# A graph layer's feed groups: ScalarE in place of VectorE makes the one-hots with which node scores are looked up

## The reference

```
h = relu(layernorm(x))
edge_h = concat([h[src], edge_attr], axis=1)
edge_m = edge_h @ a.T
edge_e = exp(-leaky_relu(edge_m @ a_2[0], 0.2))
e_rowsum = segment_sum(edge_e, src)            # 0 is replaced by 1e-12
h_prime  = segment_sum(edge_e[:, None] * edge_m, src)
out = x + h_prime / e_rowsum[:, None]
```

## Time and profile before

| | |
|---|---|
| device time, median of 3 runs | 1207.09 us (1204.01 to 1208.95) |
| the profiled execution's own time | 1210.7 us |
| its span | 1208.9 us |
| mean granted TensorE clock | 0.72 of full speed |
| busy: VectorE / GpSimd / TensorE / ScalarE | 71% / 64% / 52% / 48% |

### The profile page before, as it was taken

One profiled execution on the slowest core, in us unless ns is written; L12 is line 12 of the kernel. 1 busy time (PEld: TensorE's weight loads), 2 busy tenths in 40 slices (PEclk: granted clock), 3 DMA queues, 4 the chain that ended last, 5 costly groups with the idle time before them and its releaser, 6 DMA issues. The chain is left out here.

```text
span 1208.9 us, 22334 instructions
## 1 busy us (share of the span) xinstructions
PE 626.6 (52%) x5452; PEld 528.9 (44%) x5453; DVE 857.9 (71%) x2932; ACT 585.9 (48%) x2008; POOL 768.1 (64%) x814
## 2 busy tenths in 40 slices
PE   1671018223767028211546077771275488889887
PEld 0561015223656016211535056661264477678766
DVE  5856798876858988843546999873465768834677
ACT  1664020445666040542555034982465309978656
POOL 2006737577777777777777777777777777777000
PEclk9785558556877558555677578985587559979998
DMA  9939959589895652757879385974977529399583
GB/s 299 330 135 351 369 185 331 199 251 393 262 334 160 218 165 87 247 177 267 300 247 305 103 289 185 369 255 160 363 235 232 171 82 282 124 312 289 214 269 108
DMA packets 188561, 291.76 MB, mean 241 GB/s; under 512 B 19288, under 2 KB 125879, under 8 KB 188215
## 3 DMA queue, kind: packets, MB, share of 16 engines
q1 hardware_dynamic: 143940, 162.33, 41.3%
q10 hardware_dynamic: 19442, 75.36, 18.5%
q0 software_dynamic: 25088, 53.04, 12.3%
HBM read 159.04 MB, written 131.61 MB: 240 GB/s over the span
## 5 line engine op out<-in xcount | busy, mean ns | idle before, releaser
L507 POOL DMA_INDIRECT ordered_rows<-feed,dest x784 | 761.5, 971 | 352.7 <-issue 246.2
L755 PE MATMUL psum<-back,hots 128*128 128x129 f32 x2128 | 329.3, 312 | 36.2 <-DVE hots L1056 27.1
L755 PEld LDWEIGHTS psum<-back,hots 128*128 128x128 f32 x2128 | 293.8, 218 | 76.5 <-issue 74.1
L631 ACT ACTIVATE apart<-lanes,back 128x128 bf16<-128x128 bf16 x532 | 169.4, 389 | 236.1 <-PE psum L755 197.6
L725 PE MATMUL psum<-score_parts,place_hot 128*128 128x50 bf16 x2352 | 101.1, 206 | 276.3 <-DVE place_hot L976 257.0
L588 ACT ACTIVATE feed<-feed 128x128 f32<-128x128 f32 (+1 forms) x784 | 238.7, 387 | 0.0
L725 PEld LDWEIGHTS psum<-score_parts,place_hot 128*128 128x128 bf16 x2352 | 92.5, 111 | 286.2 <-DVE place_hot L976 265.1
L976 DVE TENSOR_SCALAR place_hot<-place_rows,lane 128x1024 bf16<-128x1024 bf16 (+1 forms) x98 | 50.1, 511 | 188.6 <-SPq L378 179.0
L580 ACT ACTIVATE feed<-leaky 128x8 f32<-128x8 f32 (+1 forms) x98 | 20.4, 208 | 325.6 <-DVE leaky L1008 325.6
L985 DVE SCALAR_TENSOR_TENSOR junk<-feed,psum 128x128 bf16<-128x128 f32 x784 | 169.9, 280 | 0.0
L1039 DVE TENSOR_TENSOR acc<-acc,psum 128x387 f32 (+1 forms) x133 | 73.5, 553 | 58.8 <-PE psum L755 47.5
(11 more groups left out here) (145 smaller groups left out, 490.3 us busy)
## 6 DMA issues: line engine op xcount, KB each, us to landing
ordered_rows<-empty SPq DMA_DIRECT2D x19, 3696.0 KB, 19.6
back<-ordered_rows ACTq DMA_DIRECT2D x133, 528.0 KB
feed<-in_edge_attr SPq DMA_DIRECT2D x97, 512.0 KB
place_rows<-places SPq DMA_DIRECT2D x98, 256.0 KB, 4.9
ordered_rows<-feed,dest POOLq DMA_INDIRECT x784
self_part<-acc ACTq DMA_DIRECT2D x1, 3234.0 KB, 11.5
feed<-self_part SPq DMA_DIRECT2D x1, 3234.0 KB
out<-feed SPq DMA_DIRECT2D x6, 448.0 KB
```

The source lines that it names most:

```text
L507: pool.indirect_dma_start(out=ordered, out_offset=bass.IndirectOffsetOnAxis(ap=dest[:, n:n + 1], axis=0), in_=feed[:, n * ROW:(n + 1) * RO ...
L631: act.activation(apart[:, v * P:(v + 1) * P], lanes[:, :], ACT.Abs, bias=tags[:, u, PLACE:PLACE + 1], scale=-1.0).then_inc(apart_done, 1)
L755: last = pe.matmul(psum[:, bass.ds(outs[u], FEAT + 1)], hots[:, hot_buffer(k) * GT + u, :], back[:, n:n + FEAT + 1], start=False, stop=u = ...
```

## The change

VectorE no longer makes `place_hot`. ScalarE makes it in two instructions over 1024 elements: the absolute difference of the broadcast places and the partition's number (`lane`), then relu of one minus that, in place. For group 0 it does so after the constants, for group g+1 at the head of its `feed_group(g)`, ahead of `scale_rows(g-1)`. ScalarE waits there for `landed` and for the look-up of the group before, which reads the same buffer. TensorE's `look_up` gets a wait for `chosen_done`: VectorE has then read the scores of the group before, an order that VectorE's own sequence gave until now.

```diff
+            def place_group(g):
+
+                act.wait_ge(landed, g + 1)
+                rows = place_rows[:, bass.ds(g % PLACE_BUFS, 1), :].rearrange("p a n -> p (a n)")
+                if not isinstance(g, int) or g > 0:
+                    act.wait_ge(node_scores, g)
+                act.activation(place_hot[:, :], rows, ACT.Abs, bias=lane[:, :], scale=-1.0).then_inc(place_apart, 1)
+                act.wait_ge(place_apart, g + 1)
+                act.activation(place_hot[:, :], place_hot[:, :], ACT.Relu, bias=1.0, scale=-1.0).then_inc(place_hot_done, 1)
+
             def feed_group(g):
 
+                if not isinstance(g, int) or g < GROUPS - 1:
+                    place_group(g + 1)
                 if not isinstance(g, int) or (g > 0 and g not in LATE):
                     scale_rows(g - 1)
...
                     constants()
+                    place_group(0)
...
                 pe.wait_ge(place_hot_done, g + 1)
+                if not isinstance(g, int) or g > 0:
+                    pe.wait_ge(chosen_done, g)
...
                 dve.wait_ge(landed, g + 1)
-                dve.tensor_scalar(place_hot[:, :], place_rows[:, bass.ds(g % PLACE_BUFS, 1), :].rearrange("p a n -> p (a n)"),
-                                  lane[:, :], None, ALU.is_equal).then_inc(place_hot_done, 1)
```

More of the change, by code:

```diff
@@ L271, in gnn_kernel @@
             edge_dots place_hot_done window_hot_done chosen_done zed_done node_scores leaky_done prob_done tagged
-            dve_hot apart_done act_hot step_done rest_zero acc_done inv_done scaled_done scaledT_done scaledT_copied
+            place_apart dve_hot apart_done act_hot step_done rest_zero acc_done inv_done scaled_done scaledT_done scaledT_copied
             out_ready self_added result_done final_loaded stored""".split()
@@ L278, in gnn_kernel @@
          edge_dots, place_hot_done, window_hot_done, chosen_done, zed_done, node_scores, leaky_done, prob_done, tagged,
-         dve_hot, apart_done, act_hot, step_done, rest_zero, acc_done, inv_done, scaled_done, scaledT_done, scaledT_copied,
+         place_apart, dve_hot, apart_done, act_hot, step_done, rest_zero, acc_done, inv_done, scaled_done, scaledT_done, scaledT_copied,
          out_ready, self_added, result_done, final_loaded, stored) = (sem(n) for n in names)
```

## The result

The changed kernel takes 1223.01 us in the median of four runs (1219.44 to 1224.61), the kernel before 1207.53 (1204.01 to 1208.95): a ratio of 1.0129, 95% interval 1.0097 to 1.016. The forecast was 1225 us, range 1213 to 1240.

What follows compares the result with a forecast made beforehand. POOL's scatter pace was taken to bound 226 to 940 us, ScalarE the last pairs with feeds. Start 3, POOL -2, late one-hots -0.9, last pairs 17.1, clock 1: +18.2 on 1207.09 gives 1225 us, range 1213 to 1240.

Steps and rivals of the forecast that it cites:

- The last pairs: Last pairs with feeds, 988 to 1057 us: eight exposed ScalarE one-hots of 2.22 us, less 0.65, add 17.1 us.
- 1 for the clock: Last pairs: TensorE, less busy, may be granted a lower clock; 1 us added, bounds 0 and 14.6.
- The 0.65 us that the sum took off as free: Last pairs: ScalarE's only idle time there, before 1006.62 us, subtracted from the eight one-hots' cost.
- The rival in which TensorE at 1.2 GHz becomes the bound: Last pairs: TensorE's round takes 33.2 us against ScalarE's 28.5, three rounds, 14 us more, 1240 us; chance 12%.
- upper bound of 14.6 us for the clock: Last pairs: the most that TensorE's lower clock was said to add, referred to the 1.2 GHz rival.
- POOL's pace: POOL-paced part, 226 to 940 us: scatters freed of VectorE's `place_hot` save 2 us, bounds 0 and -5.
- The rival built on the lock: POOL-paced part: `place_hot` blocks scatters for its whole length, so 36 us come off POOL's part, 1191 us; chance 3%.
- The start: Groups 6 and 10: ScalarE's one-hots ahead of scaling delay POOL's start by 3 us, bounds 0 and 6.
- the 12 to 14 foretold: Before group 10: POOL's second gap, 10.04 us before the change, expected at 12 to 14 us.
- VectorE's two late one-hots: Groups 87 and 88, late in the program: VectorE's only relieved instructions on the chain there, -0.9 us.
- The waits for `landed` and the reserve: POOL-paced pairs: ScalarE's new waits cost nothing; group 62's thinnest reserve, 11.6 us, isn't used up by 4.4 us of one-hots.
- the read-back foretold for 1074 to 1078 us: End of the last pairs with feeds: start of ScalarE's read-back for chunk 3, at 1057.67 us before the change.

Runs made afterwards that it cites:

- The undoing: Changed kernel with the look-up one-hots of groups 89 to 97 back on VectorE, ScalarE keeping 0 to 88: 1204.80 us, 0.9989 of the kernel before.
- the complement: Kernel before with ScalarE making the one-hots of groups 89 to 97 alone, VectorE all others: 1223.76 us, ratio 1.0147.
- the half dose: Changed kernel with one ScalarE instruction instead of two for groups 89 to 97, output not the reference's: 1211.59 us, 1.0039 of the kernel before.

## Why the prediction was right, step by step

**The last pairs: right.** Forecast 17.1 us and 1 for the clock; measured 88.24 - 69.97 = 18.3. With VectorE's one-hots the stretch took 68.35 to 69.97 us in six profiled kernels, with ScalarE's pairs 87.32 to 88.40 in three, so the 18.3 is good to 1 or 2 us. Eight pairs at 2.13 us are 17.0. The 0.65 us that the sum took off as free was not filled; it became two waits for TensorE:

```profile
1006.84 1.28 ACT L643 ACTIVATE apart<-lanes,back 128x128 bf16<-128x128 bf16 x4 [1.30 <-PE psum L770]
...
1063.72 1.28 ACT L643 ACTIVATE apart<-lanes,back 128x128 bf16<-128x128 bf16 x4 [0.85 <-PE psum L770]
```

That is 1.5 us more, on the side where the prediction put 1 for the clock. The undoing, the complement and the half dose show the cause: ScalarE's busy time in this stretch. The rival in which TensorE at 1.2 GHz becomes the bound fell: the clock did drop from 0.94 to 0.80, but the round took 28.19 us, ScalarE's sum (28.5), not TensorE's 33.2. (The prediction's upper bound of 14.6 us for the clock doesn't follow from that rival's own sum: three rounds of 33.2 less 28.5 are 14.1.)

**POOL's pace: right in sign, undersized.** Forecast -2 us. Over 560 scatters the pitch fell by 0.0058 us, -3.2 us. With VectorE still at it up to group 88, the mean scatter stayed at 968 ns; wherever ScalarE made the middle groups' one-hots, or VectorE made 8 elements, it was 963 or 964. The rival built on the lock wanted 36 us and got 3: VectorE's instruction does slow scatters, but nearly all of its length passes beside them, so that a block for its whole length, as the prediction put it, doesn't happen here.

**The start: right part, oversized as a whole.** The cost was worked out as 3.7 us behind look-up 6; the rows (TensorE, then ScalarE) show 162.91 to 172.74, 9.8 us, where 5.7 were the earlier trace rows:

```profile
162.91 1.18 PE L740 MATMUL psum<-score_parts,place_hot 128*128 128x50 bf16 x24
```

```profile
164.18 1.15 ACT L597 ACTIVATE place_hot<-place_rows,lane 128x1024 bf16<-128x1024 bf16 x1 [31.70 <-PE psum L740]
165.36 1.06 ACT L599 ACTIVATE place_hot<-place_hot 128x1024 bf16<-128x1024 bf16 x1
167.83 1.15 ACT L597 ACTIVATE place_hot<-place_rows,lane 128x1024 bf16 x1 [1.41 <-PE psum L740]
...
170.30 2.44 ACT L588 ACTIVATE feed<-feed  x8
```

Behind look-up 10 scaling ended after 6.1 us before (218.54 to 224.66) and ends after 9.8 now (215.00 to 224.84), 3.7 us more, as worked out. First before, then after:

```profile
218.54 1.18 PE L725 MATMUL psum<-score_parts,place_hot 128*128 128x50 bf16 x24 [3.78 <-DVE table L933]
...
222.21 2.45 ACT L588 ACTIVATE feed<-feed  x8
```

```profile
215.00 1.18 PE L740 MATMUL psum<-score_parts,place_hot 128*128 128x50 bf16 x24 [3.79 <-DVE table L948]
...
222.40 2.44 ACT L588 ACTIVATE feed<-feed  x8
```

But the look-ups came earlier, look-up 6 by 3.1 us (162.91 for 166.01) and look-up 10 by 3.5, where the prediction allowed 0.7 for earlier sorting. So group 10's scatter moved by 0.2 us only. POOL's second gap was 8.87 us, not the 12 to 14 foretold, because group 6 also was scattered 1.05 us later. Part of the earlier look-ups is no effect of the change: two kernels whose start is VectorE's as before (ScalarE with groups 89 to 97, or 21 to 88) began group 10's scatter at 223.85 and 224.28 us, the profiled execution of before at 225.81. Against the mean of these three, 224.65, the change costs 1.4 us, not 3; against each of them, 0.2 to 2.2.

**VectorE's two late one-hots: right.** Forecast -0.9; from group 87's start to look-up 88 it was 46.92 us (940.84 to 987.76) and is 45.94 (939.33 to 985.27).

**The waits for `landed` and the reserve: right.** POOL has no gap behind group 10. The reserve of group 62, the thinnest that the prediction found, is now:

```profile
741.32 2.43 ACT L588 ACTIVATE feed<-feed 128x128 f32<-128x128 f32 x8
```

```profile
754.49 0.96 POOL L507 DMA_INDIRECT ordered_rows<-feed,dest  x1 [0.30 <-issue]
```

10.7 us, where 11.6 were the earlier trace rows.

**The sum against one execution.** The terms as measured, 18.3 - 3.2 + 1.4 - 1.0 = 15.5 us, are the difference of the medians, 15.5. That they meet so closely is luck, since each is read from single executions that lie 1 or 2 us apart. The forecast of 18.2 was high by a start put at 3 us instead of 1.4 and by a gain of POOL's put at 2 instead of 3.2.

In the two profiled executions the read-back foretold for 1074 to 1078 us came at 1073.50, 15.8 us later than before, mainly because the start moved by 0.2 us in them and not by 3. POOL's gain did not reach VectorE whole: at group 80's first scatter it was 3.0 us (936.27 for 939.31), at VectorE's start on group 87 1.5, since the landing of the last scatter before it, for which SyncE waits, took 3.81 us where 2.29 were the earlier trace rows:

```profile
935.01 3.81 DMA ordered_rows<-feed,dest
```

The two spans differ by 12.0 only. In the part behind chunk 3's read-back, which the change doesn't touch, before took 151.2 us and after 147.4 (1208.9 - 1057.67 and 1220.9 - 1073.50). There the profiled execution of before was a late one: the eight experiments took 146.8 to 149.6.

## What to carry to other kernels

An engine's share of the whole span says little about what one more microsecond costs on it. ScalarE could take 89 groups' one-hots for nothing (0.9989, 0.9976 to 1.0001), because POOL set the pace, and nine groups' cost some 17 us, because there it was already busy for 96% of a round (20.91 of 21.8 us). Look for the stretches in which the receiving engine ends last, and move the work everywhere but there. Here these are the last pairs and, for 1 or 2 us, the start, where POOL waits for ScalarE's scaling; the version that spares both (groups 21 to 88) took 0.9961 (0.9946 to 0.9976) of the time before. When an engine is relieved, ask first what of its work stands in the chain: of 27.9 us taken off VectorE some 6 came back.

## What the runs showed of the hardware

A comparison of 1024 elements on VectorE, half a microsecond every ten, made GpSimd's scatters 4 to 6 ns longer on average (968 or 969 ns for 963 or 964), although a single scatter beside it took 0.22 us more. With 8 elements, 244 ns every ten microseconds, the mean scatter was 964 ns.
